# Host-side transposes, image scores as extra score columns, transposed probabilities two heads ahead, and a finish that shares the projections' bank

## The chip, the cores and the metric

The kernel runs on one NeuronCore of a Trainium2 chip. The metric is the device time of one launch in microseconds. Before the change it is 840.43 us, the median of 3 runs (840.39 to 840.55).

TensorE (PE) multiplies matrices and writes its results to PSUM, eight banks here. VectorE (DVE) and ScalarE (ACT) read PSUM and write SBUF; GpSimd (POOL) works from SBUF alone; SyncE (SP) issues most of the DMAs. Each engine has its own instruction list and takes it in order, and the lists meet only at semaphores.

## The reference

It is a cross attention with an added image branch, for 16 batches, 20 heads of 16 channels, 112 queries (`x`: 16 x 112 x 320) and 375 context rows (`ctx`: 16 x 375 x 512) of which the last 4 are image tokens. Cut to what matters:

```
q = x @ W_q;  k_t, v_t = text @ W_k, text @ W_v         # text: 371 rows
probs_t  = softmax(q k_t^T * scale)                     # per head 112 x 371
text_out = probs_t @ v_t
k_ip, v_ip = ip @ W_k_ip, ip @ W_v_ip                   # ip: 4 rows
sem      = l2norm(probs_t @ text) . l2norm(ip)          # per head 112 x 4
probs_ip = softmax(q k_ip^T * scale + 0.5 * sem) * mask
out      = (text_out + probs_ip @ v_ip) @ W_out + b_out + x
```

## The kernel before, in words

Most products are of float16 pairs: a float32 value is split into a high part (a float16 copy, by ACT) and a low part (the remainder, by DVE). So a tile of PSUM that is to be multiplied further is first read by ACT (`..._hi`), then by DVE (`..._lo`), and its bank is free when DVE is done. The norm of `probs_t @ text` is taken through the Gram matrix of the text (`gram`), so the per-head work is as follows.

Each head `h` of batch `b` needs on PE: `scores` (one matmul into `ps_score[h % 2]`), `transposes` (three float32 transposes of the probabilities into the single bank `ps_pT`), and `products` (Gram products into `ps_gram[h % 2]`, values into `ps_val`, and last the matmul of line 576, 4 columns wide, that gives the head's image scores). ACT takes the exponentials (`exps`), `pT_hi` (`probs_hi`) and a halved copy (`halve`); DVE takes the row minimum (`minimum`), `pT_lo` (`probs_lo`) and the quadratic form (`quadratic`); POOL takes `dual`.

Every engine's list is written out by hand, batch by batch (`all_batches`, `body`), head by head. In iteration `h` PE issues `scores` of head h+3, `transposes` of head h+1, `products` of head h, and then what else hangs at that head. DVE's iteration `h` is `minimum` of head h+3, `probs_lo` of head h+1, then the extras, then `quadratic` of head h. ACT's is `probs_hi` of head h+1, the extras, `exps` of head h+3, `halve` of head h+1.

Three kinds of extras hang at the heads, on PE at the end of iteration `h` and on ACT and DVE in iteration `h + 1`:

- `make` (lines 467 to 518): the ten pieces of the next batch's q, k, values and Gram matrix, one at every even head (`MAKE_STEP`), all in the single bank `ps_prep`; the next piece waits for DVE's `make_lo` of the piece before.
- `turn` (lines 450 to 465): three pieces of the context and one of x of the batch after next, each turned by float32 transposes on PE, at heads 1, 3, 5 and 11, in the bank `ps_light`. ACT and DVE then split them.
- `finish` (lines 579 to 595): four steps of the batch before (transpose the image probabilities, multiply by the image values, transpose the attention output, multiply by `W_out`), at heads 13, 15, 17 and 18, also in `ps_light`.

In setup the first two batches are turned over four banks, and the image rows are turned by PE as well (line 604).

Of the kernel before, what the change touches and what calls it, by code (L numbers as in the profile page):

```python
# [28 lines left out]
HALF_W = OW + HH * NIP  # L29
# [16 lines left out]
NX = 4  # L46
PIECES_TEXT, PIECE_X = (0, 1, 2), 3
TURN_STEP = {1: 0, 3: 1, 5: 2, 11: 3}

NF = 4  # L50
FINISH_STEP = {13: 0, 15: 1, 17: 2, 18: 3}
# [11 lines left out]
K_IP_STEP, RESIDUAL_STEP = 1, 19  # L63
# [4 lines left out]
T_PAD = NT * P  # L68


def channels(j):
    return P if j < CC - 1 else CR
# [15 lines left out]
def build(nc, x, ctx, mask, w_q, w_k, w_v, w_k_ip, w_v_ip, w_out, b_out, out):  # L88
    scratch = nc.dram_tensor("v_ip_scratch", (B * NIP, C), F32, kind="Internal").ap()
    stack = ExitStack()  # L90
    with stack:
# [40 lines left out]
        ctx_sb = sb("ctx_sb", [TC, NT, E])  # L132
        x_sb = [sb(f"x_sb{i}", [S, CC * P]) for i in range(2)]
# [16 lines left out]
        low = sb("low", [S, 4])  # L150
        prob = sb("prob", [S, 4, T])
        pT_hi = sb("pT_hi", [TC, 2, NT, S_PAD], F16)
        pT_lo = sb("pT_lo", [TC, 2, NT, S_PAD], F16)
# [4 lines left out]
        half_sb = [sb(f"half_sb{i}", [S, 2, HALF_W]) for i in range(2)]  # L158

        vals = sb("vals", [S, H, VW])  # L160
# [14 lines left out]
        ps_pT = ps("ps_pT", [P, 512])  # L175
# [3 lines left out]
        ps_light = ps("ps_light", [P, 512])  # L179
# [6 lines left out]
        s_ctx0 = [sem(f"s_ctx0_{i}") for i in range(NT)]  # L186
# [11 lines left out]
        s_turn, s_turn_hi, s_turn_lo = sem("s_turn"), sem("s_turn_hi"), sem("s_turn_lo")  # L198
        s_xbias, s_kip = sem("s_xbias"), sem("s_kip")

        s_score, s_low, s_prob = sem("s_score"), sem("s_low"), sem("s_prob")
        s_pT, s_pT_hi, s_pT_lo = sem("s_pT"), sem("s_pT_hi"), sem("s_pT_lo")
# [9 lines left out]
        TURN_BANKS = (*ps_score, ps_pT, ps_light)  # L212
# [35 lines left out]
        def _(sp):  # L248
            def load_ctx(a):

                sp.wait_ge(s_turn, NX * (a.n - 1) + PIECES_TEXT[-1] + 1)
                sp.dma_start(ctx_sb[:, :, :], ctx[a.n, :, :].rearrange("(c p) e -> p c e", p=TC)).then_inc(s_ctx, 16)

            def load_x(a):

                reached(sp, s_turn, NX * (a.n - 2) + PIECE_X + 1)
                reached(sp, s_xbias, a.n - 1)
                sp.dma_start(x_sb[a.odd][:, 0:C], x[a.n, :, :]).then_inc(s_x[a.odd], 16)
# [23 lines left out]
            for c in range(NT):  # L282
                sp.dma_start(ctx_sb[:, c, :], ctx[0, c * TC:(c + 1) * TC, :]).then_inc(s_ctx0[c], 16)
            sp.wait_ge(s_zero, 1)
            load_x(Batch(0, 0, 0))
            for n in range(NIP):
                sp.dma_start(ip_rows[n * B:(n + 1) * B, :], ctx[:, TX + n, :]).then_inc(s_ip, 16)
            load_context_weight(sp, 2)
            load_context_weight(sp, 1)
            load_x(Batch(1, 1, 0))  # L290
# [21 lines left out]
        def _(pool):  # L312
            for x_ in x_sb:
                nc.gpsimd.memset(x_[:, C:CC * P], 0.0)
# [33 lines left out]
            def residual(a):  # L348
                pool.wait_ge(s_x[a.odd], 16 * (a.pair + 1))
                reached(pool, s_fin_ev, NF * (a.n - 1))  # L350
                nc.gpsimd.tensor_tensor(x_bias[a.odd][:, :], x_sb[a.odd][:, 0:C], bias_sb[:, :], ALU.add).then_inc(s_xbias, 1)
# [8 lines left out]
            pool.wait_ge(s_setup_ev, 3)  # L360
# [6 lines left out]
            residual(Batch(0, 0, 0))  # L367

            def duals(b, h):
# [3 lines left out]
                nc.gpsimd.tensor_tensor(dual[:, h % 2, :], prob[:, h % 4, 0:TX], prob_16[:, h % 2, :], ALU.subtract).then_inc(s_dual, 1)  # L373

            def sum_values(f, half):

                pool.wait_ge(s_half, 2 * f.n + half + 1)
                o = half_sb[f.odd][:, half, 0:OW].rearrange("s (h w) -> s h w", w=2 * VW)
# [25 lines left out]
            def body(b, prepare, turning, finishing):  # L404
                for h in range(H):
# [15 lines left out]
                    if prepare and h == RESIDUAL_STEP:  # L421
                        residual(b.next())
# [9 lines left out]
        def _(pe):  # L432
# [11 lines left out]
            def light_bank_free(turned, finished):  # L444

                reached(pe, s_turn_lo, turned)
                reached(pe, s_turn_hi, turned)
                reached(pe, s_fin_ev, finished)

            def turn(a, k, banks=(ps_light,)):  # L450

                bank = banks[k % len(banks)]
                if k in PIECES_TEXT:
                    i = k - PIECES_TEXT[0]
                    if isinstance(a.n, int) and a.n == 0:
                        pe.wait_ge(s_ctx0[i], 16)
                    elif i == 0:
                        pe.wait_ge(s_ctx, 16 * a.n)
                    for e in range(EC):
                        last = nc.tensor.transpose(bank[:, e * TC:(e + 1) * TC], ctx_sb[:, i, e * P:(e + 1) * P], ident[0:TC, 0:TC])  # L460
                else:
                    pe.wait_ge(s_x[a.odd], 16 * (a.pair + 1))
                    for c in range(CC):
                        last = nc.tensor.transpose(bank[:, c * S:(c + 1) * S], x_sb[a.odd][:, c * P:(c + 1) * P], ident[0:S, 0:S])
                last.then_inc(s_turn, 1)

# [646 lines left out]
```

## Time and profile before

| | |
|---|---|
| median of 3 runs | 840.43 us |
| the profiled execution | 839.78 us |
| its span | 838.1 us |
| PE busy | 798.9 us (95%) |
| DVE busy | 685.0 us (82%) |
| ACT busy | 563.0 us (67%) |
| POOL busy | 405.9 us (48%) |
| granted TensorE clock, mean of the span | 0.991 |

The span is the time from the first to the last instruction of the profiled execution; the execution's own time is 1.7 us more. Matmuls overlap in the array, so the time that a matmul costs is not its duration but the distance from its start to the next start. Starts are therefore what is read below. In ACT's and DVE's rows too the next instruction often starts before the duration of the last has run out.

### The profile page before, as it was taken

How to read it: one execution, taken by the hardware profiler on the slowest of the kernel's cores; microseconds unless marked ns; L12 is line 12 of the kernel's file. 1: busy time of each engine (PE TensorE's matmuls, PEld its weight loads, DVE VectorE, ACT ScalarE, POOL GpSimd, SP SyncE). 2: the span in 40 equal slices, each digit the busy share in tenths (PEclk: the TensorE clock that was granted, in tenths of full speed). 3: DMA queues.
4: the chain of work that ended last, by engine and by line, in shares of the span. 5: the costliest groups of instructions: out<-in, count | busy, mean ns of one | idle time of the engine just before them, and what ended most of it. 6: DMA issues, size and time to landing. Idle time of an engine off the chain costs nothing.

```text
span 838.1 us, 24219 instructions
## 1 busy us (share of the span) xinstructions
PE 798.9 (95%) x8294; PEld 626.5 (75%) x8294; DVE 685.0 (82%) x2003; ACT 563.0 (67%) x1366; POOL 405.9 (48%) x516
## 2 busy tenths in 40 slices
PE   3989999999999999999999999999999999999983
PEld 2667778787787878778787877878787787877662
DVE  3777888887888888788888878888887888878893
ACT  2366767776677777667777766777776677767660
POOL 4123463645546364554536455453645545364652
PEclk9999999999999999999999999999999999999996
DMA  7322221121212112121211212121121212011000
GB/s 202 95 71 68 62 63 50 50 81 43 67 42 61 52 51 80 43 66 44 63 50 50 81 42 74 37 63 50 51 80 42 73 39 62 14 47 40 8 2 14
DMA packets 62947, 47.62 MB, mean 57 GB/s; under 512 B 10314, under 2 KB 56762, under 8 KB 62826
## 3 DMA queue, kind: packets, MB, share of 16 engines
q1 hardware_dynamic: 59898, 42.71, 19.3%
q10 hardware_dynamic: 2928, 3.36, 1.4%
q8 instruction: 68, 1.11, 0.6%
q14 instruction: 53, 0.43, 0.2%
HBM read 18.38 MB, written 2.38 MB: 25 GB/s over the span
## 4 chain that ended last, share of the span: by engine, by line
PE 92%; DVE 2%; issue 2%; DMA 1%; ACT 1%; POOL 1%; POOLq 0%; SPq 0%; DVEq 0%; ACTq 0%
PE ps_prep L438 18%; PE ps_gram L553 18%; PE ps_pT L535 14%; PE ps_gram L554 11%; PE ps_score L527 6%; PE ps_prep L511 5%; PE ps_light L438 3%; PE ps_light L460 2%; PE ps_val L561 2%; PE ps_val L563 2%; DMA ctx_sb<-in_ctx 1%; PE ps_light L586 1%; PE ps_prep L507 1%; PE ps_prep L489 1%; PE ps_prep L491 1%
## 5 line engine op out<-in xcount | busy, mean ns | idle before, releaser
L373 POOL TENSOR_TENSOR dual<-prob 112x371 f32<-112x371 f32 x320 | 277.9, 868 | 391.0 <-ACT prob L737 369.2
L553 PE MATMUL ps_gram<-gram_hi,pT_hi 125*128 125x371 f16 (+1 forms) x960 | 303.9, 320 | 0.0
L731 ACT ACTIVATE pT_hi<-ps_pT 125x336 f16<-125x336 f32 x320 | 145.4, 454 | 165.3 <-PE ps_pT L535 157.6
L554 PE MATMUL ps_gram<-gram_lo,pT_hi 125*128 125x371 f16 (+2 forms) x960 | 255.9, 267 | 0.0
L891 DVE TENSOR_REDUCE low<-ps_score 112x1 f32<-112x371 f32 x320 | 172.6, 540 | 66.8 <-PE ps_score L527 64.4
L724 ACT ACTIVATE prob<-ps_score,low 112x371 f32<-112x371 f32 x320 | 184.1, 576 | 59.9 <-DVE low L891 59.3
L896 DVE TENSOR_TENSOR pT_lo<-ps_pT,pT_hi 125x336 f16<-125x336 f32 x320 | 160.5, 502 | 31.7 <-ACT pT_hi L731 26.1
L906 DVE CUSTOM_DVE_ANT_0 quad_junk<-ps_gram,dual 112x371 f32<-112x371 f32 x320 | 170.5, 533 | 4.7 <-POOL dual L373 1.8
L535 PE MATMUL ps_pT<-ident,prob 112*125 112x112 f32 x960 | 160.4, 275 | 7.8 <-DVE pT_lo L896 2.6
L561 PE MATMUL ps_val<-val,pT_hi 125*128 125x42 f16 (+1 forms) x960 | 166.9, 182 | 0.0
L535 PEld LDWEIGHTS ps_pT<-ident,prob 112*125 112x125 f32 x960 | 140.2, 188 | 35.4 <-issue 22.2
L737 ACT ACTIVATE prob<-prob 112x371 f16<-112x371 f32 x320 | 166.0, 519 | 0.0
L563 PE MATMUL ps_val<-val,pT_lo 125*128 125x21 f16 (+1 forms) x960 | 157.5, 172 | 0.0
L561 PEld LDWEIGHTS ps_val<-val,pT_hi 125*128 125x128 f16 (+1 forms) x960 | 90.1, 96 | 55.3
L563 PEld LDWEIGHTS ps_val<-val,pT_lo 125*128 125x128 f16 (+1 forms) x960 | 90.1, 97 | 19.9
L527 PE MATMUL ps_score<-k_st,q_st 128*128 128x371 f16 x320 | 102.6, 321 | 0.6 <-DVE val L829 0.6
L553 PEld LDWEIGHTS ps_gram<-gram_hi,pT_hi 125*128 125x128 f16 (+1 forms) x960 | 96.5, 101 | 3.9
L554 PEld LDWEIGHTS ps_gram<-gram_lo,pT_hi 125*128 125x128 f16 (+1 forms) x960 | 93.0, 97 | 2.2
L383 POOL TENSOR_TENSOR nrm<-nrm,minus_half 112x5 f32<-112x5 f32 x64 | 74.9, 1171 | 1.7 <-DVE nrm L919 1.6
L438 PE MATMUL ps_prep<-w_hi,text_lo 128*128 128x320 f16 x184 | 55.0, 299 | 0.0
L438 PE MATMUL ps_prep<-w_lo,text_hi 128*128 128x320 f16 x184 | 54.9, 299 | 0.0
L438 PE MATMUL ps_prep<-w_hi,text_hi 128*128 128x320 f16 x184 | 54.9, 298 | 0.0
(198 smaller groups left out, 1444.6 us busy)
## 6 DMA issues: line engine op xcount, KB each, us to landing
ctx_sb<-in_ctx SPq DMA_DIRECT2D x15, 750.0 KB
k_st<-k_hi SPq DMA_DIRECT2D x64, 70.3 KB, 2.1
k_st<-k_lo SPq DMA_DIRECT2D x62, 70.3 KB, 2.1
q_st<-q_hi SPq DMA_DIRECT2D x64, 48.0 KB, 1.9
k_st<-k_hi SPq DMA_DIRECT2D x64, 46.9 KB, 2.0
k_st<-k_lo SPq DMA_DIRECT2D x62, 46.9 KB, 2.0
q_st<-q_lo SPq DMA_DIRECT2D x60, 48.0 KB, 2.0
x_sb<-in_x SPq DMA_DIRECT2D x16, 140.0 KB, 2.2
```

The lines of the kernel that those rows point to most:

```text
L373: nc.gpsimd.tensor_tensor(dual[:, h % 2, :], prob[:, h % 4, 0:TX], prob_16[:, h % 2, :], ALU.subtract).then_inc(s_dual, 1)
L438: last = nc.tensor.matmul(dst, parts_l(a, c), parts_r(b_, c), start=(n == 0), stop=(n == total - 1))
L535: last = nc.tensor.transpose(ps_pT[0:TC, i * S:(i + 1) * S], prob[:, h % 4, i * TC:(i + 1) * TC], ident[0:S, 0:S])
L553: nc.tensor.matmul(ps_gram[h % 2][:, 0:TX], hi, gh[0:TROWS[i], i, :], start=(i == 0), stop=False, skip_group_check=True)
L554: last = nc.tensor.matmul(ps_gram[h % 2][:, i * TC:TX], hi, gl[0:TROWS[i], i, i * TC:TX], start=False, stop=(i == NT - 1), skip_group_chec ...
L561: nc.tensor.matmul(ps_val[:, o:o + 2 * VW], pT_hi[0:r, h % 2, i, :], v[0:r, i, h, :], start=(i == 0), stop=False, skip_group_check=True)
L563: nc.tensor.matmul(ps_val[:, o:o + VW], pT_lo[0:r, h % 2, i, :], v[0:r, i, h, 0:VW], start=False, stop=(i == NT - 1), skip_group_check=True)
L724: nc.scalar.activation(prob[:, h % 4, 0:TX], ps_score[h % 2][0:S, 0:TX], ACT.Exp, bias=low[:, h % 4:h % 4 + 1], scale=-1.0).then_inc(s_pro ...
L737: nc.scalar.activation(prob_16[:, h % 2, :], prob[:, h % 4, 0:TX], ACT.Copy, scale=0.5).then_inc(s_prob_16, 1)
L891: nc.vector.tensor_reduce(low[:, h % 4:h % 4 + 1], ps_score[h % 2][0:S, 0:TX], AX.X, ALU.min).then_inc(s_low, 1)
L896: nc.vector.tensor_tensor(pT_lo[:, h % 2, :, 0:S], ps_pT[0:TC, 0:NT * S].rearrange("p (c s) -> p c s", s=S), pT_hi[:, h % 2, :, 0:S], ALU. ...
L906: nc.vector.tensor_tensor_reduce(out=quad_junk[:, h % 2, :], in0=ps_gram[h % 2][0:S, 0:TX], in1=dual[:, h % 2, :], scale=1.0, scalar=0.0, ...
```

## The change

The host hands in x and the context transposed as well (`x_t`, `ctx_t`), and the image rows in both layouts (`ip`, `ip_t`). All `turn` steps on PE go; `split_hi` and `split_lo` split the context and x straight from SBUF, in five pieces. The image scores become columns 371 to 374 of the scores matmul, and ACT copies them out of the score bank after the exponentials, once a head. `ps_light` is given up: its bank becomes the second `ps_pT`, and `finish` moves into `ps_prep`. Scores run four heads ahead, transposes two. The last finish step moves from head 18 to 19, its evacuation by DVE to head 0 of the next batch, its store to ACT's head 1. In the last batch, which prepares nothing, the finish steps stay at 13, 15, 17 and 18.

```diff
-TURN_STEP = {1: 0, 3: 1, 5: 2, 11: 3}
+SPLIT_STEP = {1: 0, 3: 1, 5: 2, 7: 3, 11: 4}
-FINISH_STEP = {13: 0, 15: 1, 17: 2, 18: 3}
+FINISH_STEP = {13: 0, 15: 1, 17: 2, 19: 3}
+STORE_STEP = 1
+LAST_FINISH_STEP = {13: 0, 15: 1, 17: 2, 18: 3}
-K_IP_STEP, RESIDUAL_STEP = 1, 19
+K_IP_STEP, RESIDUAL_STEP = 1, 11
+SCORES_AHEAD, TURNS_AHEAD = 4, 2
+PROBS, TURNED = 6, 3
...
-        ps_pT = ps("ps_pT", [P, 512])
+        ps_pT = [ps(f"ps_pT{i}", [P, 512]) for i in range(2)]
-        ps_light = ps("ps_light", [P, 512])
...  # SP
             def load_ctx(a):
-                sp.wait_ge(s_turn, NX * (a.n - 1) + PIECES_TEXT[-1] + 1)
+                sp.wait_ge(s_split_hi, NX * (a.n - 1) + PIECES_TEXT[-1] + 1)
+                sp.wait_ge(s_split_lo, NX * (a.n - 1) + PIECES_TEXT[-1] + 1)
...
                 if turning:
                     load_ctx(b.next().next())
-                    load_x(b.next().next())
+                    load_xt(b.next().next())
...
                     stack_kq(b.next())
+                    load_x(b.next())
...  # PE
-            def make(a, k, banks=(ps_prep,)):
+            def make(a, k, banks=(ps_prep,), at=0):
...
                 reached(pe, s_prep_lo, NM * a.n + k + 1 - len(banks))
+                reached(pe, s_fin_ev, NF * (a.n - 2) + sum(step < at for step in FINISH_STEP))
...  # scores
                 reached(pe, s_prob, g - 1)
-                nc.tensor.matmul(ps_score[h % 2][:, 0:TX], q_st[b.odd][:, h // 2, h % 2, :], k_st[b.odd][:, h // 2, 0:TX],
+                reached(pe, s_ip_score, g - 1)
+                nc.tensor.matmul(ps_score[h % 2][:, 0:T], q_st[b.odd][:, h // 2, h % 2, :], k_st[b.odd][:, h // 2, :],
...  # transposes
-                reached(pe, s_pT_lo, g)
+                reached(pe, s_pT_lo, g - 1)
...  # products
-                nc.tensor.matmul(ps_val[:, OW + hh * NIP:OW + (hh + 1) * NIP], q_st[b.odd][:, h // 2, h % 2, :],
-                                 k_st[b.odd][:, h // 2, TX:T], start=True, stop=True, skip_group_check=True).then_inc(s_val, 1)
-
-            def finish(f, k):
-
+
+            def finish(f, k, made):
+
+                pe.wait_ge(s_prep_lo, made)
+                reached(pe, s_fin_ev, NF * f.n + k)
...  # PE's body
                     products(b, h)
                     if prepare and h in MAKE_STEP:
-                        make(b.next(), MAKE_STEP[h])
-                    if turning and h in TURN_STEP:
-                        light_bank_free(turned, finished)
-                        turn(b.next().next(), TURN_STEP[h])
-                        turned = turned + 1
-                    if finishing and h in FINISH_STEP:
-                        light_bank_free(turned, finished)
-                        finish(b.last(), FINISH_STEP[h])
-                        finished = finished + 1
+                        make(b.next(), MAKE_STEP[h], at=h)
+                    if finishing and h in finish_step:
+                        finish(b.last(), finish_step[h], NM * (b.n + 1) + (sum(step < h for step in MAKE_STEP) if prepare else 0))
...  # ACT
+            def split_hi(a, k, first=False):
...
+                    last = nc.scalar.activation(text_hi[a.odd][:, k, 0:T], ctx_sb[:, k, :], ACT.Copy)
...  # exps, after the exponentials
+                nc.scalar.activation(ip_score[b.odd][:, h, :], ps_score[h % 2][0:S, TX:T], ACT.Copy).then_inc(s_ip_score, 1)
...  # ACT's body
+                    if turning and h in SPLIT_STEP:
+                        split_hi(b.next().next(), SPLIT_STEP[h])
...
+                    if h == STORE_STEP and b.n >= 2:
+                        store(b.last().last())
...  # DVE's body
                 for h in range(H):
-                    if h + 3 < H:
-                        minimum(b, h + 3)
+                    if h + SCORES_AHEAD < H:
+                        minimum(b, h + SCORES_AHEAD)
                     elif prepare:
-                        minimum(b.next(), h + 3 - H)
+                        minimum(b.next(), h + SCORES_AHEAD - H)
                     softly(h, 0)
-                    if h + 1 < H:
-                        probs_lo(b, h + 1)
+                    if h + TURNS_AHEAD < H:
+                        probs_lo(b, h + TURNS_AHEAD)
                     elif prepare:
-                        probs_lo(b.next(), 0)
+                        probs_lo(b.next(), h + TURNS_AHEAD - H)
+                    if h == 0 and b.n >= 2:
+                        finish(b.last().last(), NF - 1)
                     if prepare and h - 1 in MAKE_STEP:
                         make_lo(b.next(), MAKE_STEP[h - 1])
-                    if turning and h - 1 in TURN_STEP:
-                        turn_lo(b.next().next(), TURN_STEP[h - 1])
-                    if finishing and h - 1 in FINISH_STEP:
-                        finish(b.last(), FINISH_STEP[h - 1])
+                    if turning and h - 1 in SPLIT_STEP:
+                        split_lo(b.next().next(), SPLIT_STEP[h - 1])
+                    if finishing and h - 1 in finish_step:
+                        finish(b.last(), finish_step[h - 1])
```

## Rows read from the trace of the kernel before

**Rows 1.** Windows: stretch; length, busy us of each engine, clock, DMA.

```profile
147.05:195.89 48.84, 48.70 (x519) 38.66 (x518) 41.56 (x124) 34.72 (x86) 24.69 (x31) 1.00 0.21 56
...
814.00:819.00 5.00, 4.21 (x46) 3.39 (x43) 3.21 (x11) 1.26 (x5) 3.50 (x4) 1.00 0.01 3
819.00:828.00 9.00, 0.38 (x1) 0.14 (x1) 4.35 (x17) 0.82 (x2) 4.07 (x5) 0.70 0.05 16
```

**Rows 2.** Chain of waits: start us, us; the last finish step, batches 13 and 14.

```profile
728.78 1.22 PE ps_light L438 x9
...
777.02 1.22 PE ps_light L438 x9
```

**Rows 3.** Timeline of PE, batch 2: end of head 1, a turn, head 2.

```profile
149.65 0.16 PE L576 MATMUL ps_val<-k_st,q_st 128*128 128x4 f16 x1
149.68 0.63 PE L460 MATMUL ps_light<-ident,ctx_sb 125*128 125x125 f32 x4
150.14 0.32 PE L527 MATMUL ps_score<-k_st,q_st 128*128 128x371 f16 x1
```

**Rows 4.** Timeline of PE, start of head 10, after a head without extras.

```profile
169.57 0.32 PE L527 MATMUL ps_score<-k_st,q_st 128*128 128x371 f16 x1
...
169.93 0.55 PE L535 MATMUL ps_pT<-ident,prob 112*125 112x112 f32 x3
```

**Rows 5.** Timeline of PE, head 13, its finish step, start of head 14.

```profile
177.85 0.32 PE L527 MATMUL ps_score<-k_st,q_st 128*128 128x371 f16 x1
...
179.29 0.27 PE L583 MATMUL ps_light<-ident,fprob 112*80 112x112 f32 x1
179.40 0.32 PE L527 MATMUL ps_score<-k_st,q_st 128*128 128x371 f16 x1
179.66 0.55 PE L535 MATMUL ps_pT<-ident,prob 112*125 112x112 f32 x3
```

**Rows 6.** Timeline of ACT and DVE in head 13.

```profile
178.52 0.45 ACT L731 ACTIVATE pT_hi<-ps_pT 125x336 f16<-125x336 f32 x1 [0.83 <-PE ps_pT L535]
...
179.00 0.51 DVE L896 TENSOR_TENSOR pT_lo<-ps_pT,pT_hi 125x336 f16<-125x336 f32 x1 [0.25 <-ACT pT_hi L731]
...
180.51 0.28 DVE L832 SCALAR_TENSOR_TENSOR gram_lo<-ps_prep,gram_lo 125x125 f16<-125x125 f32 x1
```

**Rows 7.** Timeline of PE: the starts of heads 15, 17 and 19.

```profile
182.10 0.32 PE L527 MATMUL ps_score<-k_st,q_st 128*128 128x371 f16 x1
...
186.52 0.32 PE L527 MATMUL ps_score<-k_st,q_st 128*128 128x371 f16 x1
...
192.58 0.32 PE L527 MATMUL ps_score<-k_st,q_st 128*128 128x371 f16 x1
```

**Rows 8.** Timeline of DVE: last reads of ps_prep and ps_light in batch 2.

```profile
150.25 1.04 DVE L829 SCALAR_TENSOR_TENSOR q_lo<-ps_prep,q_mask,q_hi 128x336 f16<-128x336 f32 x2 [0.35 <-ACT q_hi L699]
...
182.04 0.26 DVE L976 COPY fprob_T<-ps_light 80x112 f32<-80x112 f32 x1
...
184.51 0.28 DVE L832 SCALAR_TENSOR_TENSOR gram_lo<-ps_prep,gram_lo 125x125 f16<-125x125 f32 x1
...
188.74 0.28 DVE L832 SCALAR_TENSOR_TENSOR gram_lo<-ps_prep,gram_lo 121x121 f16<-121x121 f32 x1
...
190.26 0.49 DVE L983 TENSOR_TENSOR attn_lo<-ps_light,attn_hi 128x336 f16<-128x336 f32 x1
...
194.16 0.48 DVE L829 SCALAR_TENSOR_TENSOR val<-ps_prep,val 121x320 f16<-121x320 f32 x1
```

**Rows 9.** Timeline of the last batch, head 18, and the finish step behind it.

```profile
815.70 0.16 PE L576 MATMUL ps_val<-k_st,q_st 128*128 128x4 f16 x1
815.86 0.50 DVE L983 TENSOR_TENSOR attn_lo<-ps_light,attn_hi 128x336 f16<-128x336 f32 x1
...
816.61 0.31 PE L438 MATMUL ps_light<-wo_hi,attn_hi 128*112 128x320 f16 x1 [0.75 <-DVE attn_lo L983]
```

**Rows 10.** Groups of instructions on ACT: the smallest activation.

```profile
L749 ACT ACTIVATE fexp<-fused 112x80 f32<-112x80 f32 x16 | 4.1, 258 | 6.2 <-DVE fused L960 6.2
```

More of the change, by code:

```diff
@@ L28 @@
 OW = HH * 2 * VW
-HALF_W = OW + HH * NIP
 EPS = 1e-12
@@ L297, in _ @@
             load_rows(sp, wo_sb, w_out, s_wo)
+            load_x(Batch(0, 0, 0))
             def body(b, prepare, turning, finishing):
@@ L420, in body @@
                         batch_k_ip(b.next())
-                    if prepare and h == RESIDUAL_STEP:
-                        residual(b.next())
+                    if h == RESIDUAL_STEP:
+                        residual(b)
             def tail(b):
@@ L442, in _ @@
             w = (w_hi, w_lo)
[L444 to L465, printed above, removed]
-            def make(a, k, banks=(ps_prep,)):
+            def make(a, k, banks=(ps_prep,), at=0):
                 bank = banks[k % len(banks)]
@@ L610, in _ @@
                 make(start, k, SETUP_BANKS)
-            pe.wait_ge(s_setup_ev, 1)
+            pe.wait_ge(s_ip, 32)
             pe.wait_ge(s_w[2], 16)
-            light_bank_free(NX, 0)
             for j in range(CC):
                 for e in range(EC):
-                    last = nc.tensor.matmul(ps_light[0:channels(j), j * 64:(j + 1) * 64], w_raw[:, e, 2, j * P:j * P + channels(j)],
+                    last = nc.tensor.matmul(ps_pT[1][0:channels(j), j * 64:(j + 1) * 64], w_raw[:, e, 2, j * P:j * P + channels(j)],
                                             ip_T[:, e, :], start=(e == 0), stop=(e == EC - 1))
             last.then_inc(s_setup_pe, 1)
-            pe.wait_ge(s_setup_ev, 3)
-            for k in range(NX):
-                turn(second, k, TURN_BANKS)
             pe.wait_ge(s_const, 3)
@@ L632, in _ @@
             pe.wait_ge(s_ipdiag, 1)
-            light_bank_free(2 * NX, 0)
-            nc.tensor.matmul(ps_light[0:S, 0:64], ones[:, :], ip_diag[:, :], start=True, stop=True).then_inc(s_setup_pe, 1)
+            pe.wait_ge(s_setup_ev, 2)
+            nc.tensor.matmul(ps_pT[1][0:S, 0:64], ones[:, :], ip_diag[:, :], start=True, stop=True).then_inc(s_setup_pe, 1)
             scores(start, 0)
@@ L675, in _ @@
         def _(act):
-            def turn_hi(a, k, banks=(ps_light,)):
-                bank = banks[k % len(banks)]
-                act.wait_ge(s_turn, NX * a.n + k + 1)
+            def split_hi(a, k, first=False):
                 if k in PIECES_TEXT:
-                    i = k - PIECES_TEXT[0]
-                    last = nc.scalar.activation(text_hi[a.odd][:, :, i * TC:(i + 1) * TC],
-                                                bank[:, 0:EC * TC].rearrange("p (e t) -> p e t", t=TC), ACT.Copy)
-                else:
-                    last = nc.scalar.activation(x_hi[:, :, :].rearrange("p c s -> p (c s)"), bank[:, 0:CC * S], ACT.Copy)
-                last.then_inc(s_turn_hi, 1)
+                    if first:
+                        act.wait_ge(s_ctx0[k], 16)
+                    elif k == 0:
+                        act.wait_ge(s_ctx, 16 * a.n)
+                    if k == 0:
+                        reached(act, s_prep, NM * (a.n - 1))
+                    last = nc.scalar.activation(text_hi[a.odd][:, k, 0:T], ctx_sb[:, k, :], ACT.Copy)
+                else:
+                    act.wait_ge(s_xt[a.odd], 32 * (a.pair + 1))
+                    reached(act, s_prep, NM * (a.n - 1) + PIECE_Q + 1)
+                    last = nc.scalar.activation(x_hi[:, :, :], xt_sb[a.odd][:, :, :], ACT.Copy)
+                last.then_inc(s_split_hi, 1)
             def make_hi(a, k, banks=(ps_prep,)):
@@ L729, in probs_hi @@
                 act.wait_ge(s_pT, g + 1)
-                reached(act, s_val, g - 1)
-                nc.scalar.activation(pT_hi[:, h % 2, :, 0:S], ps_pT[0:TC, 0:NT * S].rearrange("p (c s) -> p c s", s=S), ACT.Copy).then_inc(s_pT_hi, 1)
+                reached(act, s_val, g + 1 - TURNED)
+                nc.scalar.activation(pT_hi[:, g % TURNED, :, 0:S], ps_pT[h % 2][0:TC, 0:NT * S].rearrange("p (c s) -> p c s", s=S), ACT.Copy).then_inc(s_pT_hi, 1)
             def halve(b, h):
@@ L743, in half_out @@
                     reached(act, s_soft, SOFT * (b.n - 2) + SOFT_ARGS)
-                nc.scalar.activation(half_sb[b.odd][:, half, :], ps_val[0:S, 0:HALF_W], ACT.Copy).then_inc(s_half, 1)
+                nc.scalar.activation(half_sb[b.odd][:, half, :], ps_val[0:S, 0:OW], ACT.Copy).then_inc(s_half, 1)
             def fin_exp(f):
@@ L769, in _ @@
             for k in range(NX):
-                turn_hi(start, k, TURN_BANKS)
+                split_hi(start, k, first=True)
             split_weight(wq_hi[:, :, :], wq_sb[:, :, :], s_wq, 2)
@@ L813, in body @@
                         fin_exp(b.last())
-                    if finishing and h == H - 1:
+                    if not prepare and h == H - 1:
                         store(b.last())
@@ L1052, in _ @@
             minimum(start, 2)
+            probs_lo(start, 1)
+            minimum(start, 3)
             split_weight(3, wo_lo[:, :, :], wo_sb[:, :, :], wo_hi[:, :, :])
```

220 lines of the change are left out of this document (112 added, 108 removed).

## The prediction

> **What bounds the kernel now.** I read the windows first. In a steady batch PE is busy in 48.70 of 48.84 us, while DVE has 41.56 and ACT 34.72 [rows 1]; the reader is to see that PE is the only engine without room. The chain of waits says the same: its long pieces are all PE's, and they repeat with the period of a batch, 48.84 us for batches 1 to 13. Batch 14, which turns nothing, takes 777.02 - 728.78 = 48.24 [rows 2]. Last I read the timeline of PE by starts, since a modelled busy time hides short waits, and the timelines of ACT and DVE beside it, to see how far each is behind PE at each head. A profile's busy shares can't show what decides this case: who has to be done before PE's next instruction.
>
> **What leaves PE.** Head 1's image matmul starts at 149.65 and the turn behind it at 149.68, so that matmul costs 0.03 (0.025 before rounding); the turn ends with the next scores at 150.14: 0.46 us [rows 3]. A batch has three such turns, 1.38, and one of x with three narrower transposes, 0.32 by the same cost per column: 1.70 in all. The 20 image matmuls give 0.50, and 80 more score columns take back 80 / 371 of the 0.16 between a scores matmul and the transposes: 0.03. So 0.47.
>
> Then the single bank of the transposes. Behind a head that made nothing, the transposes start 0.36 after the scores [rows 4] instead of 0.16, since they wait for DVE's `pT_lo` of the head before, and take 0.07 longer, as their weights could not be loaded ahead. There are three such heads, and two milder ones, of which head 14 waits 0.26 [rows 5]; I count 1.1 us a batch. With two banks the wait is for two heads back, which DVE has long done. That this stall is real shows in batch 14: its three text turns and the x turn are gone, worth 1.70, and it is only 0.60 shorter. What is late next is nothing on PE's side in heads 1 to 12: a pair of heads with a piece of k has 4.7 us of PE's time, against 3.5 to 4.5 on DVE and ACT.
>
> PE's own work in a batch is thus 48.84 - 1.70 - 0.47 - 1.1 = 45.57 us.
>
> **What the shared bank adds.** This is where I expect the time to go. `make` of piece k ends PE's iteration of an even head. ACT and DVE read the piece in their iteration of the next, odd head, behind `probs_hi` and behind `minimum` and `probs_lo`, and all of these read what PE issues at the start of that same odd head. Before, nobody on PE asked for the piece until the end of the next even head. Now the finish step stands at the end of the odd head and waits for the whole bank, and the next `make` waits for the finish step's read, which hangs in the same way at the even head. PE's queue is in order, so scores and transposes of the next head, and with them everybody, stand behind the waiting instruction.
>
> The times, from the start of head 13 at 177.85. PE reaches the finish step at 179.29, 1.44 later, 1.42 without the image matmul [rows 5]. But ACT's `pT_hi` starts at 178.52, DVE's `pT_lo` at 179.00, and DVE's last read of the Gram piece ends at 180.51 + 0.28 = 180.79, 2.94 after the head began [rows 6]. From a DVE end to PE's start I take 0.15: `pT_lo` ends at 179.51 and the waiting transposes start at 179.66 [rows 5, 6]; in the last batch it was 0.25 [rows 9]. The wait at head 13 is 2.94 + 0.15 - 1.42 = 1.67. In the same way, from starts in [rows 7] and ends in [rows 8]: head 15, 184.79 - 182.10 = 2.69, wait 1.42; head 17, 189.02 - 186.52 = 2.50, wait 1.23; head 19, 194.64 - 192.58 = 2.06, wait 0.79.
>
> At the even heads DVE reaches its extra 1.58 after the head's start (194.16 - 192.58 [rows 7, 8]). The copy of `fprob_T` takes 0.26 and the other three steps about the 0.49 of `attn_lo` [rows 8]. So head 14 waits 1.84 + 0.15 - 1.42 = 0.57, and heads 16, 18 and 0 of the next batch 0.80 each. The eight waits are 8.08 us. They don't overlap with one another, since PE restarts each time from the same line, with the others waiting for it.
>
> The trace already holds one such pair. In the last batch two finish steps stand at heads 17 and 18. PE is through with head 18 at 815.73, DVE's `attn_lo` of that very head ends at 816.36, and PE goes on at 816.61: 0.88 us lost [rows 9], where my working for a read of that length gives 0.80.
>
> One smaller wait of the kind: the q piece is read until 151.29, 3.06 after head 1 began at 148.23, and without the turn PE asks for the bank after two heads, 2.84: 0.37 with the 0.15 [rows 3, 8].
>
> Bounds: were the semaphore free, the nine waits would be 1.35 a batch less; at 0.25 each they are 0.9 more. PE's 45.57 could be 0.4 off to either side.
>
> **What I cost at nothing.** ACT's 20 copies of 4 columns, in no row: each is between a few hundredths and the 0.26 of the smallest activation, 80 columns [rows 10], at most 5.2 us a batch, in an engine with 14 us free [rows 1]; they stand behind the exponentials, which have signalled by then. Uncovered they would cost up to that much. The five splits replace four turns' reads of the same elements, now from SBUF; a piece of 375 columns should cost as a read of 371 from PSUM. POOL's residual moves from head 19 to 11, beside idle POOL time. On SP the text load now waits for both splits, which are done at head 8, and x is loaded behind the restacking DMAs, a head's reading of it ahead by half a batch; transposed rows are shorter packets, but DMA is 21% busy [rows 1]. Scores of the next batch at head 16 instead of 17 need the restacked k, whose DMAs follow head 8. The store at head 1 waits for a read at head 0. None of this is near PE.
>
> Setup loses two rounds of turning, some 3.4 us of PE's time, but weights and DVE pace it; I take 2, between 0 and 5. Batch 0 has no finish and gains 1.70 + 0.47 + 1.1 - 0.37, about 3. The last batch gains its 20 matmuls, 0.5; its finish steps meet no `make`.
>
> **The sum.** A full batch: 45.57 + 8.08 + 0.37 = 54.02, or 5.18 more than 48.84; 13 of them give 67.3. Batch 14: 54.02 less the two waits that need a following `make` (0.80 and 0.37) is 52.85, 4.6 more than 48.24. Together 67.3 + 4.6 - 3 - 0.5 - 2 = 66.4. The span of 838.1 becomes 904.5, the profiled execution's own time 906.2 (it was 839.8), and as the median of 3 runs was 0.6 above that execution, about 906.
>
> **A rule weighed.** In the stretch 814 to 819, where PE waits like this, the granted clock is 1.00, the 2.4 GHz level; it is 0.70 in the stretch behind it, after PE had been idle for microseconds in a row [rows 1]. None of my waits is longer than 1.7 us, so I keep the clock. The Trainium skill, "TensorE: Matmul & The Clock Gate", section "A second HAM failure mode: psum-queue depth-cycling", says that frequent short idling between groups of matmuls can make the clock swing between its levels. By that rule this change would hurt far more; it is the third rival below.
>
> **The rivals.**
>
> 1. Faster: two banks and the lead of two heads let ACT and DVE run so far ahead that the bank is free when PE asks. Then only 45.57 + 0.37 = 45.94 is left, 2.9 less for 13 batches, 2.7 less for batch 14, and 5.5 at the ends: about 795 us. For it speaks that the waits on `ps_pT` really go. Against it: `minimum` of head h+4 and `probs_lo` of h+2 stand ahead of the extra in DVE's list and read what PE issues in that same iteration, so neither can lead PE there.
> 2. Slower, but by half: DVE frees the bank in time for the next `make`, and only the four waits of the finish steps stay, 5.11. A batch is 51.05, and the time about 866. Against it is the 0.88 in the last batch [rows 9].
> 3. The clock falls in the stretch with the waits. Heads 13 to 18 alone are 192.58 - 177.85 = 14.7 us of PE's time [rows 5, 7]; at 1.2 GHz that is 14.7 more in 14 batches, over 1,100 us.
> 4. ACT's copies get onto the path, at the full 0.26: 320 of them, 83 us, about 990.
>
> **Chances.** Forecast 0.86, rival 1 0.06, rival 2 0.04, rivals 3 and 4 0.02 each. The forecast's own bounds (1.35 less and 0.9 more in 14 batches, 0.4 a batch on PE's work, setup) reach from about 885 to 924, and I give 887 to 923. A measurement of this kernel can tell 0.2% from no change. Faster by more than that 0.06, within it 0.01, slower 0.93.
>
> **What would show it.** In the changed trace: a batch of about 54 us; PE idle ahead of L583, L586, the transposes of `attn` and the first product with `wo`, released by DVE's `gram_lo` or `val`, and ahead of the pieces made at heads 14, 16, 18 and 0, released by DVE's `fprob_T`, `attn`, `attn_lo` and `out_sb`, 0.5 to 1.7 us each; no wait of the transposes for `pT_lo`; heads without extras at 1.42 us; clock 1.00. I am wrong if the finish steps start right behind their head's products, if a batch takes 46 us, or if the waits come in other heads than 13 to 0.

## The result, and the profile after

The changed kernel takes 901.03 us, the median of 4 executions, against 840.41 for the kernel before on the same chip: 1.072 times as long, with a 95% interval of 1.070 to 1.074. The forecast was 906, in a range of 887 to 923. The profiled execution took 900.71 us (before 839.78), its span is 898.9 (before 838.1), so the difference to explain is 60.8 us of span. The ratio leaves out one of the four executions, which took 1141.18 us, about the price that rival 3 named, at a mean granted clock of 0.655 where the others had 0.985 to 0.991; it left no trace, so its cause is open.

The page first: the busy times, and the chain of waits by engine.

```profile
PE 769.8 (86%) x7730; PEld 602.0 (67%) x7730; DVE 704.4 (78%) x2018; ACT 575.1 (64%) x1702; POOL 420.3 (47%) x516
...
PE 36%; DVE 28%; issue 16%; POOL 10%; ACT 8%; DMA 1%; ACTq 1%; DVEq 0%; SPq 0%; POOLq 0%
```

PE has 29 us less work than before, and the kernel is 61 us slower: no engine has 90% of the span any more. The chain that ended last was 92% PE's before; now only 36% of it is, and it changes between PE and DVE. That is how a loss by waiting looks: every busy share falls.

The windows say how much per batch (length; busy us of PE, PEld, DVE, ACT and POOL; clock, DMA share, GB/s). In the chain a piece of 27 matmuls for q stands once in each batch, and from the first of these to the last are 13 batches:

```profile
361.28:415.20 53.92, 47.18 (x482) 37.10 (x482) 43.12 (x125) 35.48 (x106) 25.63 (x31) 1.00 0.21 54
```

```profile
91.84 1.34 PE ps_prep L451 x27
...
792.70 1.49 PE ps_prep L451 x27
```

A steady batch takes 53.92 us at clock 1.00 where it took 48.84 [rows 1], and (792.70 - 91.84) / 13 = 53.91 is the mean. The view of waits (engine, tile and line waiting <- what released it: us in total, times, longest) names the places, 14 times each:

```profile
PE ps_prep L576 <- DVE gram_lo L823: 21.1, 14, 1.6
...
PE ps_prep L579 <- DVE gram_lo L823: 15.3, 14, 1.1
...
PE ps_prep L583 <- DVE gram_lo L823: 13.9, 14, 1.0
...
PE ps_prep L451 <- DVE attn_lo L971: 9.2, 14, 0.7
...
PE ps_prep L451 <- DVE val L820: 7.7, 14, 0.6
...
PE ps_prep L497 <- DVE fprob_T L964: 5.9, 14, 0.4
```

L576, L579 and L583 are the first three finish steps; the rest are the last finish step (released by `val`) and the pieces made at heads 14 and 18. The pieces at heads 16 and 0 wait as well, but the view puts their waits down to `issue` (8.3 and 9.2 us) and not to DVE's `attn` and `out_sb`, as the prediction had it; in the kernel with the sharing alone, below, it names these two. The wait of the transposes for `pT_lo` [rows 4, 5] is gone.

Heads 13 and 14 one by one. PE, the start of head 13, its finish step, head 14 and the piece behind it:

```profile
390.26 0.32 PE L518 MATMUL ps_score<-k_st,q_st 128*128 128x375 f16 x1
...
393.38 0.29 PE L576 MATMUL ps_prep<-ident,fprob 112*80 112x112 f32 x1 [1.55 <-DVE gram_lo L823]
393.51 0.33 PE L518 MATMUL ps_score<-k_st,q_st 128*128 128x375 f16 x1
...
395.50 0.38 PE L497 MATMUL ps_prep<-text_lo,text_hi 128*128 128x125 f16 x4 [0.42 <-DVE fprob_T L964]
```

And DVE from head 13 to head 15:

```profile
390.38 0.75 DVE L832 TENSOR_TENSOR x_lo<-xt_sb,x_hi 128x336 f16<-128x336 f32 x1
...
391.52 0.53 DVE L880 TENSOR_REDUCE low<-ps_score 112x1 f32<-112x371 f32 x1
391.97 0.49 DVE L885 TENSOR_TENSOR pT_lo<-ps_pT,pT_hi 125x336 f16<-125x336 f32 x1
...
393.05 0.27 DVE L823 SCALAR_TENSOR_TENSOR gram_lo<-ps_prep,gram_lo 125x125 f16<-125x125 f32 x1
...
394.67 0.51 DVE L885 TENSOR_TENSOR pT_lo<-ps_pT,pT_hi 125x336 f16<-125x336 f32 x1 [0.26 <-ACT pT_hi L717]
395.10 0.26 DVE L964 COPY fprob_T<-ps_prep 80x112 f32<-80x112 f32 x1
...
396.95 0.55 DVE L880 TENSOR_REDUCE low<-ps_score 112x1 f32<-112x371 f32 x1 [1.14 <-PE ps_score L518]
```

The reader is to see DVE's order: the minimum of head 17, `pT_lo` of head 15, and only then the Gram piece, ended at 393.32; PE asked for the bank at 390.26 + 1.42 = 391.68 and started at 393.38, 1.70 later. At head 14 the same with a read of 0.26: end 395.36, start 395.50, 0.57 after PE was ready.

Two things make DVE late here, and the prediction named one. At heads 15, 17 and 19 DVE stands idle for 1.14, 0.83 and 1.67 us until PE's scores come, as the last row shows for head 15: there the order alone makes its read late. At head 13 it has no gap between 389.39 and 393.24. It is still at head 12's work, the split of x and the quadratic form, when the scores of head 17 are ready, so a part of this wait, the longest, is DVE's backlog. The last three experiments turn on it.

### The profile page after: what moved, and what is told of

It reads as the page before. It is cut to its first block, busy times and chain, and to the rows that moved or that the text cites. A ratio compares the mean times of both kernels' runs of the same rounds, so it can differ in the third digit from the quotient of the medians.

```text
span 898.9 us, 23808 instructions
## 1 busy us (share of the span) xinstructions
PE 769.8 (86%) x7730; PEld 602.0 (67%) x7730; DVE 704.4 (78%) x2018; ACT 575.1 (64%) x1702; POOL 420.3 (47%) x516
## 4 chain that ended last, share of the span: by engine, by line
PE 36%; DVE 28%; issue 16%; POOL 10%; ACT 8%; DMA 1%; ACTq 1%; DVEq 0%; SPq 0%; POOLq 0%
PE ps_prep L451 11%; POOL nrm L396 6%; PE ps_pT L526 6%; POOL dual L386 4%; PE ps_gram L544 4%; DVE low L880 4%; DVE pT_lo L885 4%; ACT pT_hi L717 3%; PE ps_score L518 3%; DVE quad_junk L895 3%; PE ps_gram L545 2%; PE ps_prep L501 2%; DVE val L820 2%; DVE gram_lo L820 1%; PE ps_prep L579 1%
## 5 line engine op out<-in xcount | busy, mean ns | idle before, releaser
L386 POOL TENSOR_TENSOR dual<-prob 112x371 f32<-112x371 f32 x320 | 283.1, 885 | 446.2 <-ACT prob L723 417.5
L723 ACT ACTIVATE prob<-prob 112x371 f16<-112x371 f32 x320 | 168.5, 527 | 0.0
L526 PE MATMUL ps_pT<-ident,prob 112*125 112x112 f32 x960 | 154.5, 269 | 0.8 <-ACT prob L707 0.8
L526 PEld LDWEIGHTS ps_pT<-ident,prob 112*125 112x125 f32 x960 | 145.4, 189 | 9.9 <-issue 2.8
L518 PE MATMUL ps_score<-k_st,q_st 128*128 128x375 f16 x320 | 103.2, 323 | 2.5 <-ACT ip_score L711 2.3
L396 POOL TENSOR_TENSOR nrm<-nrm,minus_half 112x5 f32<-112x5 f32 x64 | 83.2, 1301 | 1.2 <-DVE nrm L908 0.9
L711 ACT ACTIVATE ip_score<-ps_score 112x4 f32<-112x4 f32 x320 | 56.7, 177 | 0.0
L451 PE MATMUL ps_prep<-w_hi,text_lo 128*128 128x320 f16 x184 | 54.9, 299 | 0.0
```

Of the source, the lines that this page charges most:

```text
L386: nc.gpsimd.tensor_tensor(dual[:, h % 2, :], prob[:, g % PROBS, 0:TX], prob_16[:, h % 2, :], ALU.subtract).then_inc(s_dual, 1)
L451: last = nc.tensor.matmul(dst, parts_l(a, c), parts_r(b_, c), start=(n == 0), stop=(n == total - 1))
L526: last = nc.tensor.transpose(ps_pT[h % 2][0:TC, i * S:(i + 1) * S], prob[:, g % PROBS, i * TC:(i + 1) * TC], ident[0:S, 0:S])
```

## The experiments

All are compared with the kernel before, which took 840.07 to 840.45 us on these chips. The wait of PE in front of an extra (a piece or a finish step) is read throughout as here: the extra's start, less the start of its head's scores, less the 1.42 us that a head takes without extras.

**A bank of its own for the finish.** `finish` goes back to a bank of its own, at the price of the second `ps_pT`; everything else of the change stays.

```diff
-        ps_pT = [ps(f"ps_pT{i}", [P, 512]) for i in range(2)]
+        ps_pT = [ps("ps_pT0", [P, 512])] * 2
+        ps_light = ps("ps_light", [P, 512])
...  # transposes
-                reached(pe, s_pT_lo, g - 1)
+                reached(pe, s_pT_lo, g)
...  # make
-                reached(pe, s_fin_ev, NF * (a.n - 2) + sum(step < at for step in FINISH_STEP))
...  # finish
-                pe.wait_ge(s_prep_lo, made)
```

> The changed kernel, but the finish steps have a bank of their own again, and the transposed probabilities share one. Theory A (PE waits for ACT and DVE to read the shared bank): the eight waits of 7.7 us a batch go, the waits of the transposes for pT_lo come back with about 1.1; a batch takes 47.3 us instead of 53.9 and the kernel about 811 us (800 to 822). Theory B (the loss comes from the 20 image copies on ACT and the splits from SBUF, which all stay): 890 us or more.

Measured: 830.49 us, 0.988 of before (0.986 to 0.990); a batch takes 48.6. The eight waits for the shared bank are gone, so the sharing is what costs. But it is 20 us above the expectation, outside its range, and the view of waits shows why (its row for PE's transposes, and under it PE's timeline at one of them):

```profile
PE ps_pT L526 <- DVE pT_lo L884: 17.0, 34, 1.2
```

```profile
396.69 0.32 PE L518 MATMUL ps_score<-k_st,q_st 128*128 128x375 f16 x1
...
397.37 0.55 PE L526 MATMUL ps_pT<-ident,prob 112*125 112x112 f32 x3 [0.36 <-DVE pT_lo L884]
```

The transposes start 0.68 after the scores here, not 0.16; at 411.19 it is 1.00. In the batch from 389.05 on eight heads start them too late, by 2.42 us in all, and in each of the eight they take 0.07 longer, 0.56: 3.0 together. In a batch of the kernel before it is five heads, 0.73 and 0.35, 1.1 together. The odd heads up to 11, which held the turns, now hold nothing, so at each even head from 2 to 12 PE comes to the transposes before `pT_lo` of the head before is done. Taking 2.17 us of PE's work out of a batch (1.70 of turns and 0.47 of image matmuls) made it 0.2 shorter.

**The shared bank's readers first, on both engines.** In every head ACT and DVE read `ps_prep` before anything else.

```diff
...  # DVE's body; ACT's in the same way
                 for h in range(H):
+                    if h == 0 and b.n >= 2:
+                        finish(b.last().last(), NF - 1)
+                    if prepare and h - 1 in MAKE_STEP:
+                        make_lo(b.next(), MAKE_STEP[h - 1])
+                    if finishing and h - 1 in finish_step:
+                        finish(b.last(), finish_step[h - 1])
                     if h + SCORES_AHEAD < H:
                         minimum(b, h + SCORES_AHEAD)
```

> The changed kernel with its banks as they are, but ACT and DVE read the projections' bank first in each head, ahead of pT_hi, minimum and pT_lo. Theory A (the place of the reads in the two lists makes the waits): a read starts with the end of the piece and not with the transposes of the next head; the waits behind the Gram pieces shrink to 0.7, 0.5 and 0.4 us, the others go; a batch takes 47.5 to 48.5 us, the kernel about 820 (810 to 835). Theory C (ACT and DVE have too much work in these heads, whatever its order): 885 us or more, with the waits moved to products or scores.

**The same on DVE alone**, with ACT's order as in the change.

> As the kernel with both reads first, but on DVE alone; ACT still reads behind pT_hi. Theory A: the waits at heads 14, 16 and 0, which hang on DVE alone, go (2.1 us a batch); those at heads 13, 15, 17, where DVE waits for ACT's part, stay, and minimum and pT_lo come later behind them; the kernel about 870 us (860 to 890). If DVE's list alone made the waits, it would come near the kernel with both first, 835 or less.

Measured: 843.09 us for both engines (ratio 1.004, 1.003 to 1.005), 913.9 for DVE alone (1.088, 1.087 to 1.090), slower than the change itself. The first took 58 us off the change's 901: nothing moved but the place of the reads in two lists, so the waits are the readers' lateness and not the bank. Both missed their ranges, the first by 23 us from its middle, the second by 44. In the first the waits at heads 13, 15 and 17 are as expected, 0.77, 0.43 and 0.32, but two more stand in each batch, 1.80 at head 10 and 0.79 at head 18. The view of waits of the second kernel, and that of the first under it:

```profile
ACT prob L707 <- DVE low L880: 219.5, 208, 2.4
...
DVE val L820 <- ACT val L699: 53.8, 34, 2.7
...
PE ps_gram L544 <- DVE quad L895: 14.6, 15, 1.1
```

```profile
ACT prob L707 <- DVE low L880: 164.8, 201, 2.3
...
PE ps_val L552 <- ACT half_sb L730: 17.0, 16, 1.2
```

After the change ACT's exponentials waited 57.0 us in all for DVE's minimum; here 165 and 220. DVE's read can't start before ACT's `..._hi` of the same piece, and with DVE alone moved, DVE's whole list stands at the read until ACT comes to it, with the minimum behind. The exponentials are then late, and so is `halve`, which is behind them on ACT; PE's values of the next half wait for it. In PE's timeline of the first kernel that wait stands at head 10:

```profile
562.80 0.19 PE L552 MATMUL ps_val<-val,pT_hi 125*128 125x42 f16 x1 [1.18 <-ACT half_sb L730]
```

In the second kernel (its mean batch is 54.6 us) the wait at head 10 is 2.5 to 2.7 us: 1.18 of it for `halve` as in the first, and 1.0 to 1.1 for DVE's quadratic form, which has to empty a `ps_gram` bank (the last row of the second kernel's view; in the first this wait is 0.2 to 0.3). Those at heads 13, 15, 17 and 18 are still 1 us or more, and only heads 14, 16 and 0 wait for nothing. How much each engine's lateness adds to the other's I did not separate.

**The sharing alone.** The kernel before, with `finish` in `ps_prep`, its last step at head 19, its last read at head 0, its store at head 1, and the change's waits on that bank. POOL's residual sum had to move with them, from head 19 of the batch before to head 1; the image matmuls, the single `ps_pT`, the leads of 3 and 1 and the turns (now alone in `ps_light`) stay as they were.

```diff
-FINISH_STEP = {13: 0, 15: 1, 17: 2, 18: 3}
+FINISH_STEP = {13: 0, 15: 1, 17: 2, 19: 3}
...  # make
+                reached(pe, s_fin_ev, NF * (a.n - 2) + sum(step < at for step in FINISH_STEP))
...  # finish, in ps_prep for ps_light
+                pe.wait_ge(s_prep_lo, made)
```

> The kernel before, with one part of the change alone: the finish shares the projections' bank, its last step at head 19, its read at head 0, the store at head 1 (and the residual sum at head 1, the bias buffer being free only then). The turns, the image matmuls and the single bank of pT stay. Theory A: the eight waits of 0.6 to 1.7 us come on top of 48.84 us, less what the old stalls overlap with; a batch takes 55.5 to 56.5 us, the kernel 935 to 950 us. Theory B: no more than 845.

Measured: 941.3 us, 1.120 of before (1.119 to 1.122). One batch is 55.53 us, at clock 1.00, 6.69 more than before, and the waits stand in the change's own places and are nearly of its size, 1.58 at head 13 and 0.48 to 1.24 at the others:

```profile
PE ps_prep L587 <- DVE gram_lo L837: 19.8, 14, 1.4
...
PE ps_prep L590 <- DVE gram_lo L837: 15.1, 14, 1.1
...
PE ps_prep L594 <- DVE gram_lo L837: 13.7, 14, 1.0
```

So the two leads and the second `ps_pT` neither make these waits nor help them much.

Not all of the 101 us is the sharing's. The first steady batch begins at 107.34 where it began at 98.22, 9.1 later, though batch 0 has no finish. That is the moved residual sum: SP loads the next x only when POOL's sum is done (57.36), and behind that load in SP's list stands the restacking of q and k, which begins at 73.28 for 64.72. At the end of batch 0 PE waits for it:

```profile
96.77 0.49 PE L529 MATMUL ps_score<-k_st,q_st 128*128 128x371 f16 x1 [6.18 <-DMA k_st<-k_lo]
```

The other 92, of which 87 lie in the 13 steady batches, are still more than the whole change costs (61).

**Ordered reads where both kinds of step stand.** From head 13 on ACT reads the bank first; DVE takes the minimum, then the bank, then `pT_lo`; its reads for the finish stand ahead of the minimum. Up to head 12 the order of the reads of a piece is the change's. ACT's `half_out` goes ahead of the exponentials.

```diff
...  # ACT's body
+                    early = h > 12
+                    if early and prepare and h - 1 in MAKE_STEP:
+                        make_hi(b.next(), MAKE_STEP[h - 1])
...  # DVE's body
+                    if finishing and h - 1 in finish_step:
+                        finish(b.last(), finish_step[h - 1])
                     if h + SCORES_AHEAD < H:
                         minimum(b, h + SCORES_AHEAD)
...
+                    if early and prepare and h - 1 in MAKE_STEP:
+                        make_lo(b.next(), MAKE_STEP[h - 1])
```

> The changed kernel with its banks, and a finer order of the lists than the kernel with both reads first: in heads 13 to 19 ACT reads the projections' bank ahead of pT_hi, DVE takes minimum, then that bank, then pT_lo; heads 1 to 12 keep the order of the changed kernel; DVE reads a finish step ahead of minimum; ACT's copy of half the values stands ahead of the exponentials. Theory A: of the waits in the kernel with both reads first, those at head 10 (1.5 us) and 18 (0.8) go and 0.8, 0.4 and 0.2 stay at heads 13, 15 and 17; a batch takes 47.2 us, the kernel about 808 us (800 to 818). Theory C (ACT and DVE have too much work there, whatever its order): 835 or more.

Measured: 817.81 us, 0.973 of before (0.972 to 0.975). It beats both kernels: 83 us under the change, with nothing changed but the order of instructions. It lies at the upper end of what was expected. The window of a batch, and PE's finish steps in the batch before it:

```profile
428.10:476.05 47.95, 46.42 (x486) 36.83 (x484) 42.19 (x125) 36.37 (x107) 25.76 (x30) 1.00 0.24 61
```

```profile
411.36 0.29 PE L576 MATMUL ps_prep<-ident,fprob 112*80 112x112 f32 x1 [0.90 <-DVE gram_lo L826]
...
415.85 0.79 PE L579 MATMUL ps_prep<-vip_diag,fprob_T 80*112 80x320 f32 x2 [0.28 <-DVE gram_lo L826]
...
420.47 0.51 PE L583 MATMUL ps_prep<-ident,attn 112*128 112x112 f32 x3 [0.16 <-DVE gram_lo L826]
```

The waits at the even heads and at head 19 are gone; left are 1.05 at head 13, 0.43 at 15, 0.31 at 17, and 0.28 and 0.21 at heads 2 and 10. Three more kernels asked what holds head 13.

**A shorter piece there.** The Gram piece of head 12 (three reads by ACT, four by DVE) and the value piece of head 10 (one and one) change places, in the last kernel and in the change.

```diff
-PIECE_Q, PIECES_K, PIECES_V, PIECES_G = 0, (1, 2, 3), (4, 5, 9), (6, 7, 8)
+PIECE_Q, PIECES_K, PIECES_V, PIECES_G = 0, (1, 2, 3), (4, 6, 9), (5, 7, 8)
```

> As the ordered kernel, and the first Gram piece, which takes ACT and DVE longest to read, is made at head 10 and the second piece of the values at head 12, where a finish step follows. Theory A: the wait at head 13 (0.8 us) goes too; a batch takes 46.5 us, the kernel about 798 us (790 to 808). If the ordered kernel's rest of waits has another cause: no gain over it.

> The changed kernel with this exchange alone: the read ahead of the finish step of head 13 is that of a piece of the values, which ends 2.06 us after the head's start, not 2.94. Theory A: the wait at head 13 falls from 1.7 to 0.7 or 0.8 us, that of the other heads stays; 14 times 0.9 us less, about 888 us (884 to 892). If the wait is a fixed cost of sharing the bank, whatever is read from it: 901.

Measured: 824.53 us with the ordered reads (0.980, 0.979 to 0.982; 6.7 us slower than without the swap) and 907.0 in the change (1.079, 1.078 to 1.081; 6 slower). Both missed. In the first the wait at head 13 is 1.16 where it was 1.05, and a new one of 0.41 stands at head 12. In the second the wait at head 13 is 1.57 where it was 1.70, and a new one of 0.58 stands at head 12. PE's timeline there, and DVE's under it:

```profile
446.15 0.31 PE L451 MATMUL ps_prep<-w_hi,text_hi 128*128 128x320 f16 x1 [0.43 <-DVE gram_lo L823]
...
447.79 0.32 PE L518 MATMUL ps_score<-k_st,q_st 128*128 128x375 f16 x1
...
450.78 0.29 PE L576 MATMUL ps_prep<-ident,fprob 112*80 112x112 f32 x1 [1.42 <-DVE val L820]
```

```profile
447.20 0.53 DVE L880 TENSOR_REDUCE low<-ps_score 112x1 f32<-112x371 f32 x1
447.65 0.51 DVE L958 TENSOR_TENSOR fprob<-fexp,fmax 112x80 f32<-112x80 f32 x1
448.08 0.49 DVE L885 TENSOR_TENSOR pT_lo<-ps_pT,pT_hi 125x336 f16<-125x336 f32 x1
448.50 0.49 DVE L832 TENSOR_TENSOR x_lo<-xt_sb,x_hi 128x336 f16<-128x336 f32 x1
448.92 0.53 DVE L895 CUSTOM_DVE_ANT_0 quad_junk<-ps_gram,dual 112x371 f32<-112x371 f32 x1
...
449.38 0.53 DVE L880 TENSOR_REDUCE low<-ps_score 112x1 f32<-112x371 f32 x1
449.83 0.49 DVE L885 TENSOR_TENSOR pT_lo<-ps_pT,pT_hi 125x336 f16<-125x336 f32 x1
450.25 0.47 DVE L820 SCALAR_TENSOR_TENSOR val<-ps_prep,val 125x320 f16<-125x320 f32 x1
```

DVE has no gap in these rows, nor in those left out. When head 13 begins at 447.79 it has still to finish head 12's work, and comes to the minimum of head 17 at 449.38, 1.59 after the head's start, where in the change it came 1.26 after. The read is 0.46 us shorter and starts 0.33 later.

**A lighter iteration ahead of it.** The ordered kernel with the split of x at head 15.

```diff
-SPLIT_STEP = {1: 0, 3: 1, 5: 2, 7: 3, 11: 4}
+SPLIT_STEP = {1: 0, 3: 1, 5: 2, 7: 3, 15: 4}
```

> This is e5_ordered with the split of x moved from head 11 to head 15 (one number of the split's table), so that DVE carries half a microsecond less in its iteration of head 12, just ahead of the wait of 1.05 us that e5 kept at head 13. Theory: the wait left at head 13 follows DVE's own backlog at heads 11 to 13, and DVE has only the minimum of head 17 and the Gram piece to do once it is there; the split in head 12's iteration takes 0.49 to 0.75 us of DVE, so the wait falls to 0.4 to 0.6 us; heads 15 and 17 may wait 0.1 to 0.2 longer, as the split now stands ahead of head 17's read. Batch 47.96 - 0.5 + 0.15 = 47.6, so 14 x 0.35 = 5 us less: about 813 us. Rival: DVE makes up its backlog before head 13 anyway and the wait is only minimum(17) behind PE's scores plus the read; then the wait stays at 1.05 and the time is 818 or a little more, 820, by what head 17 loses.

Measured: 817.25 us, 0.9725 of before (0.971 to 0.974), as without the edit: the rival's outcome. But the reason isn't the rival's. PE's wait is 1.07 (head 13 starts at 600.39, the finish step at 602.88), and what precedes it has changed. DVE's timeline and ACT's:

```profile
598.69 0.81 DVE L958 TENSOR_SCALAR fmax<-fmax,mask_sb 112x20 f32<-112x20 f32 x1
599.41 0.53 DVE L883 TENSOR_REDUCE low<-ps_score 112x1 f32<-112x371 f32 x1
...
601.88 0.29 DVE L823 SCALAR_TENSOR_TENSOR gram_lo<-ps_prep,gram_hi 125x125 f16<-125x125 f32 x1 [0.17 <-ACT val L692]
```

```profile
599.98 0.57 ACT L707 ACTIVATE prob<-ps_score,low 112x371 f32<-112x371 f32 x1 [1.14 <-DVE low L883]
...
600.90 0.48 ACT L689 ACTIVATE gram_hi<-ps_prep 125x371 f16<-125x371 f32 x1
```

Now DVE waits 0.17 for ACT. ACT comes to the Gram piece only at 600.90, because its exponentials waited for a minimum that DVE took at 599.41, behind a step of 20 columns that lasted 0.81 here and 0.23 in the ordered kernel. From ACT's first read to DVE's last end (602.55 + 0.28) the piece takes 1.93 us, more than the 1.42 of a head. From this I estimate that with these reads in sequence a wait of 0.5 or more at head 13 would stay whatever stands ahead; it was not tried.

## Why the prediction was right, and where its terms were not

The mechanism, the places and the size were as forecast: 901.0 against 906. By its steps, in one batch (361.28 to 415.20; the wait at head 0 from 413.04 on):

| | predicted | measured |
|---|---|---|
| wait at head 13 | 1.67 | 1.70 |
| head 14 | 0.57 | 0.57 |
| head 15 | 1.42 | 1.24 |
| head 16 | 0.80 | 0.75 |
| head 17 | 1.23 | 1.14 |
| head 18 | 0.80 | 0.81 |
| head 19 | 0.79 | 0.71 |
| head 0 | 0.80 | 0.74 |
| sum of the eight | 8.08 | 7.66 |
| q piece, head 2 | 0.37 | 0.28 |
| `halve`, head 10 | none | 0.31 |
| PE's own work | 45.57 | 53.92 - 8.25 = 45.67 |
| batch | 54.02 | 53.92 |

- **The waits.** Shown by the sharing alone, which brings them, by the bank of its own, which takes them away, and by the ordered reads, which take five of eight away and shorten the rest. Rival 1 (the leads free the bank in time) and rival 2 (only four waits) fall with the rows of the change itself. The size at head 13 came out right because it was read off the kernel before, whose DVE had a backlog there too; as a cause the prediction named the order alone.
- **The single bank's stall, 1.1 us.** As a figure for the kernel before it was right: 0.73 of late starts and 0.35 of slower transposes. What the prediction did not say is that this term and the 2.17 us of turns and image matmuls are not independent. With the turns gone and the bank still single the stall is 3.0 us. The turns were filling a wait. Both went here, so the sum held; where only one went, my expectation was 20 us off.
- **The last batch** is the most mis-sized term. Forecast: 0.5 us gained. The kernel before started its heads there 1.72 us apart at the least (785.22, 786.94, 788.66), the stall of the single bank in every head, since no extra stands behind any of them; the changed one starts the first six 1.42 apart, in PE's timeline, and those from there to head 13 1.5 to 2.6:

```profile
845.45 0.32 PE L518 MATMUL ps_score<-k_st,q_st 128*128 128x375 f16 x1
...
846.87 0.32 PE L518 MATMUL ps_score<-k_st,q_st 128*128 128x375 f16 x1
```

  From the start of its head 0 to the end of the span: 838.1 - 779.52 = 58.6 before, 898.9 - 844.02 = 54.9 after, so 3.7 gained; 2.2 of it lies ahead of the start of head 13 (24.9 for 22.7), and the rest behind it was not taken apart.
- **The account of the 60.8 us.** 13 batches from the q piece at 91.84 (98.22 before) to the one at 792.70 (733.14): 700.86 - 634.92 = 65.9, forecast 67.3. The start, setup and batch 0: 6.4 gained, forecast 5. Batch 14 from there to head 0 of the last: 51.3 - 46.4 = 4.9 lost, forecast 4.6. The last batch: 3.7 gained, forecast 0.5. Together 65.9 - 6.4 + 4.9 - 3.7 = 60.7. The forecast had 66.4, 5.6 more: 1.4 in the batches, 1.4 at the start and 3.2 in the last batch, less 0.3 in batch 14, but for rounding.
- **What I cost at nothing.** ACT's 320 copies of 4 columns (56.7 us, 177 ns each) start 0.05 or 0.06 us ahead of what follows them (392.55 and 392.61, say), far under the 0.26 of the bound; in a batch ACT is busy 0.8 us more than before, and no wait on them stands in a steady batch (two, 2.3 us in all, stand in batch 0 and in the last). Rival 4 falls. The move of POOL's residual sum to head 11 was not free either: it lengthens DVE's split of x by 0.25 us just ahead of head 13, as the last section shows. What I had not looked for is `halve`: with the leads longer, PE reaches the values of head 10 before ACT has copied the last half, 0.31 a batch.
- **The clock** stayed at 1.00 in the steady batches of the profiled executions, with eight waits of 0.6 to 1.7 us in each here and of 0.5 to 1.6 in the sharing alone. All 35 timed executions of the eight kernels above had means of 0.981 and up. Rival 3 falls for the executions that the ratio counts.

## What to carry to other kernels

When two tenants share a bank, the price is set by the readers' place in their own in-order lists: write down for each hand-over when the reader comes to it, counted from the start of the head in which PE asks. What stands ahead of the read and depends on work that PE issues in that same head makes it late, and so does a backlog from the head before. Before taking work off the bounding engine, look whether it is filling a wait: 2.17 us taken from a batch gave 0.2 while the bank behind the wait stayed single. And before giving up a sharing, try the order of the reads: here it was worth 83 us, and a reader moved on one engine alone made it worse.

## What the runs showed of the hardware

Small steps of DVE are stretched by POOL. DVE's step of 80 columns at L948 takes 0.23 us at its shortest and 0.89 to 0.95 in 13 of the 16 batches, and the timelines of DVE and of POOL in the changed kernel show what it ends with:

```profile
384.38 0.95 DVE L948 TENSOR_TENSOR fused<-fused,fmax 112x80 f32<-112x80 f32 x1
```

```profile
384.34 0.89 POOL L386 TENSOR_TENSOR dual<-prob 112x371 f32<-112x371 f32 x1 [1.40 <-ACT prob L723]
```

It began 0.04 us after POOL's instruction and ended at 385.33, 0.10 after POOL's end at 385.23. In one batch the same step began ahead of POOL's, at 815.13 against 815.21, and took 0.23. L958 does the same: it started at 389.39 and ended at 390.04, with POOL's at 389.06 + 0.89 = 389.95. The Trainium skill, "SBUF — State Buffer", section "SBUF: two separate sides", says that DVE and GpSimd share a port pair that is locked for a whole instruction, and that a DVE instruction with two SBUF inputs needs it; both steps have two such inputs and `dual` reads SBUF, so these rows agree. The step of 20 columns at 598.69 above, 0.81 long, has one tensor and one column as inputs; it too stands beside a `dual`, of 598.58 to 599.47, and ends at 599.50. Why this form is stretched too is open.

The split of x, now from SBUF, lasts 0.75 us in the steady batches of the changed kernel (390.38 above), where POOL's residual sum runs beside it (389.90 to 390.76). It is not SBUF as such that makes it longer: in the kernel with the split at head 15, where POOL runs nothing beside it, it lasts 0.50, and before, from PSUM, it lasted 0.49.
